# Layer 1's leaky slope: from VectorE in layer 2's edge stage to ScalarE and GpSimd in the first merge

## The reference

```
msg = x[src] @ W_msg + edge_attr @ W_edge
agg = segment_max(msg, dst); agg = 0 where a node has no edge
c   = leaky_relu(agg + x @ W_root + b)          # slope 0.01
```

## Time and profile before

| | |
|---|---|
| median of 3 runs | 2085.36 us (2079.59 to 2089.3) |
| the profiled execution | 2083.45 us, span 2081.6 us |
| mean granted TensorE clock | 0.914 |
| busy share | PE 78%, VectorE (DVE) 63%, GpSimd (POOL) 52%, ScalarE (ACT) 51% |

### The profile page before, as it was taken

One profiled execution on the slowest core, in us unless ns is written; L12 is line 12 of the kernel. 1 busy time (PEld: TensorE's weight loads), 2 busy tenths in 40 slices (PEclk: granted clock), 3 DMA queues, 4 the chain that ended last, 5 costly groups with the idle time before them and its releaser, 6 DMA issues.

```text
span 2081.6 us, 37108 instructions
## 1 busy us (share of the span) xinstructions
PE 1620.9 (78%) x11422; PEld 1408.5 (68%) x11422; DVE 1317.8 (63%) x2383; ACT 1056.0 (51%) x2450; POOL 1092.5 (52%) x1454
## 2 busy tenths in 40 slices
PE   3888888888888888886687888888888777666664
PEld 2657766667768888885566766676667666666664
DVE  2556666656666555553465655555654789999998
ACT  1323444334433455553344444443444678898897
POOL 6755666666640000002666666666664778766673
PEclk9988999999999999998899999889989989998887
DMA  6757888798874678885566766666767789999996
GB/s 122 187 132 217 232 240 230 214 243 229 231 222 176 203 237 261 271 279 188 142 183 181 196 189 185 191 188 177 197 182 233 221 268 294 306 301 291 297 293 195
DMA packets 580028, 459.13 MB, mean 221 GB/s; under 512 B 448559, under 2 KB 487346, under 8 KB 579842
## 3 DMA queue, kind: packets, MB, share of 16 engines
q1 hardware_dynamic: 497956, 301.88, 52.0%
q10 hardware_dynamic: 50910, 97.16, 12.6%
q0 software_dynamic: 30976, 57.72, 11.6%
HBM read 283.25 MB, written 173.37 MB: 219 GB/s over the span
## 4 chain that ended last, share of the span: by engine, by line
PE 52%; DVE 19%; another core or an unknown queue 10%; issue 10%; ACT 3%; POOL 3%; DMA 2%; ACTq 1%; SPq 1%; POOLq 0%; DVEq 0%
PE ps L556 17%; PE ps L468 14%; PE ps L459 8%; PE ps L437 6%; DVE stats L933 5%; PE ps L430 4%; DVE arena L931 3%; DVE arena L928 3%; PE ps L447 3%; POOL onehot L417 2%; DMA onehot_bytes<-arena 2%; DVE arena L951 1%; DVE arena L876 1%; ACT arena L620 1%
## 5 line engine op out<-in xcount | busy, mean ns | idle before, releaser
L556 PE MATMUL ps<-hold,onehot 128*128 x4688 | 610.6, 292 | 187.0 <-POOL onehot L417 136.9
L556 PEld LDWEIGHTS ps<-hold,onehot 128*128 128x128 f32 x4688 | 579.3, 204 | 218.4 <-issue 218.3
L384 POOL DMA_INDIRECT arena<-nodes,src_perm x392 | 370.8, 946 | 581.6 <-SPq L351 356.0
L468 PEld LDWEIGHTS ps<-w_root,onehot 97*128 97x128 f32 x3136 | 437.0, 209 | 170.0 <-issue 166.0
L468 PE MATMUL ps<-w_root,onehot 97*128 97x128 f32 x3136 | 460.3, 294 | 52.9 <-ACT arena L620 32.1
L384 POOL DMA_INDIRECT arena<-in_x_dram,src_all x392 | 377.7, 964 | 232.8 <-issue 115.0
L620 ACT COPY arena<-ps 128x384 f32<-128x384 f32 x392 | 188.2, 480 | 370.8 <-remote 241.3
L417 POOL CAST onehot<-keep 128x256 f32<-128x256 uint8 x588 | 302.2, 563 | 107.6 <-PE ps L556 64.5
L862 DVE TENSOR_TENSOR_SCAN arena<-keep,arena,ps 96x512 f32<-96x512 bf16 x196 | 248.3, 1267 | 142.1 <-remote 80.1
L459 PE MATMUL ps<-ident,arena 128*96 128x128 f32 x1568 | 262.3, 291 | 34.2 <-issue 27.7
L680 ACT COPY arena<-ps 128x384 f32<-128x384 f32 x392 | 166.7, 477 | 210.4 <-PE ps L556 210.4
(11 more groups left out here) (97 smaller groups left out, 1152.7 us busy)
## 6 DMA issues: line engine op xcount, KB each, us to landing
root<-arena ACTq DMA_DIRECT2D x196, 384.0 KB
arena<-root SPq DMA_DIRECT2D x196, 384.0 KB, 4.6
nodes<-arena SPq DMA_DIRECT2D x98, 384.0 KB, 2.8
arena<-nodes SPq DMA_DIRECT2D x98, 384.0 KB
arena<-in_x_dram SPq DMA_DIRECT2D x97, 384.0 KB
arena<-in_x_dram SPq DMA_DIRECT2D x48, 768.0 KB, 8.1
out_dram<-arena SPq DMA_DIRECT2D x48, 768.0 KB, 4.7
onehot_bytes<-arena ACTq DMA_DIRECT2D x147, 128.0 KB
```

The source lines that it names most:

```text
L384: nc.gpsimd.indirect_dma_start(out=gathered[t.ring][0:t.p, i, 0:D], out_offset=None, in_=table_in, in_offset=bass.IndirectOffsetOnAxis(ap= ...
L468: last = nc.tensor.matmul(no_ps[m % 2][:, i * P:(i + 1) * P], nodes_t[m % NODE_RING][0:D + 1, i * P:(i + 1) * P], w_root[0:D + 1, layer * ...
L556: nc.tensor.matmul(ps_bytes[:, bass.ds(place_at, SLOT)].bitcast(F32), onehot[:, k % NS, i, :], flat[:, bass.ds(chunk_at, P)], start=False, ...
```

## The change

Layer 1's result gets its slope before it is stored. `evacuate` makes two activations per node group from PSUM: `Relu(-0.01 x)` into a scratch half (`sloping`, in the place of `x_in[0]`, two halves) and `Relu(x)` into `nodes_out`. GpSimd then subtracts the first from the second, a half (128 x 768) at a time, and SyncE's store waits for that (`sloped`). ScalarE waits from the third half on until GpSimd has done the half two before. In edge stage 1 the operands are plain copies and VectorE's maxima are gone.

```diff
@@ sync: store_half
-                sp.wait_ge(evacuated[0], (h + 1) * HG)
+                sp.wait_ge(sloped, h + 1)
@@ gpsimd, between layer 1's gathers and the wait for ready
+            for h in range(2 * NSB):
+                pool.wait_ge(evacuated[0], (h + 1) * HG)
+                at = slice(h % 2 * HG * C * D, (h % 2 + 1) * HG * C * D)
+                y = nodes_out[h // 2 % 3][:, at]
+                nc.gpsimd.tensor_tensor(y, y, sloping[h % 2], ALU.subtract).then_inc(sloped, 1)
@@ scalar: read_edges
-                if t.layer == 0:
-                    nc.scalar.copy(to, of).then_inc(et_done, 1)
-                else:
-                    nc.scalar.activation(to, of, ACT.Copy, scale=slopes[:, 0:1]).then_inc(scaled, 1)
+                nc.scalar.copy(to, of).then_inc(et_done, 1)
@@ scalar: read_nodes
-                    nc.scalar.activation(to, of, ACT.Copy, scale=SLOPE).then_inc(nt_scaled, 1)
+                nc.scalar.copy(to, of).then_inc(nt_done, 1)
@@ scalar: evacuate
+                    if layer == 0 and h >= 2:
+                        act.wait_ge(sloped, h - 1)
...
+                        if layer == 0:
+                            off = n % HG * C * D
+                            nc.scalar.activation(sloping[h % 2][:, off:off + C * D]..., slot[:, n % RING, :, 0:D], ACT.Relu, scale=-SLOPE)
+                        nc.scalar.activation(nodes_out[s % 3][:, at:at + C * D]..., slot[:, n % RING, :, 0:D],
+                                             ACT.Copy if layer else ACT.Relu).then_inc(evacuated[layer], 1)
@@ vector: edge_phase
-                if layer == 1:
-                    leaky_edges(EdgeGroup(layer, 0))
...
-                    if layer == 1 and g + 1 < NE:
-                        leaky_edges(EdgeGroup(layer, g + 1))
...
-                            leaky_nodes(n)
```

More of the change, by code:

```diff
@@ L104, in gnn @@
         count = sb("count", [P, P], BF16)
-        slopes = sb("slopes", [P, 1], F32)
         rows = sb("rows", [ROWS_ON + 1, TP], I32)
@@ L125, in gnn @@
         x_in = [arena[:, UNIT_RING * UW + (3 + i) * SW:UNIT_RING * UW + (4 + i) * SW] for i in range(2)]
+        sloping = [x_in[0][:, i * HG * C * D:(i + 1) * HG * C * D] for i in range(2)]
         assert HG == UG and BATCH == 2 * C and NODE_RING == 2 * NS and EDGE_RING == 4
@@ L180, in gnn @@
         keep_in = sems("keep_in", EDGE_RING)
-        ones_set, turned, scaled, et_done, em_full, scanned, eb_full, held = (sem(n) for n in (
-            "ones_set", "turned", "scaled", "et_done", "em_full", "scanned", "eb_full", "held"))
-        block_in, nt_full, nt_scaled, nt_done = sems("block_in", UNIT_RING), sem("nt_full"), sem("nt_scaled"), sem("nt_done")
+        ones_set, turned, et_done, em_full, scanned, eb_full, held = (sem(n) for n in (
+            "ones_set", "turned", "et_done", "em_full", "scanned", "eb_full", "held"))
+        block_in, nt_full, nt_done = sems("block_in", UNIT_RING), sem("nt_full"), sem("nt_done")
+        sloped = sem("sloped")
         no_full, root_read, root_stored = sem("no_full"), sem("root_read"), sems("root_stored", UNIT_RING)
@@ L608, in read_nodes @@
                 to, of = nodes_t[m % NODE_RING][0:D, :], nt_ps[m % 2][0:D, :]
-                if layer == 0:
-                    nc.scalar.copy(to, of).then_inc(nt_done, 1)
-                else:
-                    nc.scalar.activation(to, of, ACT.Copy, scale=SLOPE).then_inc(nt_scaled, 1)
+                nc.scalar.copy(to, of).then_inc(nt_done, 1)
             def read_root(layer, n):
@@ L677, in evacuate @@
                     act.wait_ge(stepped[layer], ends[h % ENDS])
+                    if layer == 0 and h >= 2:
+                        act.wait_ge(sloped, h - 1)
                     for n in range(h * HG, (h + 1) * HG):
                         at = n % SG * C * D
-                        nc.scalar.copy(nodes_out[s % 3][:, at:at + C * D].rearrange("p (j d) -> p j d", d=D), slot[:, n % RING, :, 0:D],
-                                       ).then_inc(evacuated[layer], 1)
+                        if layer == 0:
+                            off = n % HG * C * D
+                            nc.scalar.activation(sloping[h % 2][:, off:off + C * D].rearrange("p (j d) -> p j d", d=D), slot[:, n % RING, :, 0:D], ACT.Relu, scale=-SLOPE)
+                        nc.scalar.activation(nodes_out[s % 3][:, at:at + C * D].rearrange("p (j d) -> p j d", d=D), slot[:, n % RING, :, 0:D],
+                                             ACT.Copy if layer else ACT.Relu).then_inc(evacuated[layer], 1)
                 def reseed(h):
@@ L736, in _ @@
             nc.vector.memset(end_prev, N - 1)
-            nc.vector.memset(slopes[0:D, :], SLOPE)
-            nc.vector.memset(slopes[D:K, :], 1.0)
             nc.vector.memset(ones, 1.0)
@@ L842, in _ @@
                 pieces[META_AT + 2 + k] = [lambda k=k: piece_pick(k)]
[L844 to L852, removed]
             def scan(t):
@@ L885, in edge_phase @@
             def edge_phase(layer):
-                if layer == 1:
-                    leaky_edges(EdgeGroup(layer, 0))
                 for g in range(NE):
-                    if layer == 1 and g + 1 < NE:
-                        leaky_edges(EdgeGroup(layer, g + 1))
-                    groups = node_groups(layer, g)
-                    for n in groups[0:1]:
-                        if layer == 1:
-                            leaky_nodes(n)
                     scan(EdgeGroup(layer, g))
@@ L897, in edge_phase @@
                         hold_chunks(EdgeGroup(layer, g - 1))
-                    for n in groups[1:]:
-                        if layer == 1:
-                            leaky_nodes(n)
                     if layer == 0:
```

## The result

The changed kernel takes 2115.31 us (median, 2114.7 to 2122.98) where the kernel before, on the same chip, takes 2085.34 us (2079.59 to 2089.3). The ratio is 1.0147, 95% interval 1.0112 to 1.0182: slower by 30 us. The profiled execution took 2114.7 us, span 2112.9 us, mean granted TensorE clock 0.914 as before.

A forecast was written before the change was run, and what follows sets the result against it. It took TensorE's matmuls to bound the first merge and the turn of four gathers and late TensorE signals the second edge stage. 2083.45 + 40.5 + 2.8 - 14 = 2112.8, so 2113 us, range 2035 to 2160 us.

The forecast's parts named there:

- the three terms: First merge +40.5 us, end of that merge +2.8 us, second edge stage -14 us.
- The subtraction's duration: First merge, GpSimd: one subtraction of 128x768 fp32 takes 1.8 us, between bounds of 1.05 and 2.1 us.
- Merge 0, +40.5 forecast: First merge: compares and subtractions exclude each other, 302.5 us of work in a 262 us stretch, +40.5 us.
- Rival C: First merge: the subtraction or the hand-overs are dear, merge +87 us, total 2159 us; chance 0.20.
- ScalarE beside TensorE: zero: First merge: two more Relu copies per half fit beside TensorE, 2.63 of 3.0 us, zero cost, at most 8 us.
- End of the merge, +2.8: After the first merge's last half: two more copies, one subtraction and signals before the store, +2.8 us.
- Edge stage 1, -14 forecast: Second edge stage: removing VectorE's maxima gains 0.15 us in each of 92 sets of gathers, -14 us.
- the hop on the turn (82 us): Second edge stage: VectorE's maximum is part of the turn, its removal gives 0.83 us a group, 82 us.
- four fifths of 0.19 us: Second edge stage: share of mean set minus undisturbed turn, for sets that narrowly missed the signal, 0.15 us a set.
- A: Second edge stage: the hop was on the turn, gain 82 us instead of 14, total 2045 us; chance 0.18.
- B: First merge: no lock between compare and subtraction, or a cheap one, +0 to 8 us, total 2076 us; chance 0.13.

The follow-up runs named there:

- e2_merge_only: Kernel before with the changed merge 0 (Relu copies and GpSimd subtraction), its layer 2 maxima kept: ratio 1.0133, merge 0 347.0 us.
- e3_relu_only: Changed kernel without GpSimd's subtraction, both Relu copies on ScalarE kept: ratio 1.001, merge 0 321.1 us.
- e4_write_only: Changed kernel with a GpSimd iota that only writes SBUF in the subtraction's place, without Relu(-0.01 x) copies: ratio 1.0024, merge 0 326.9 us.
- e5_sub_only: Changed kernel without the Relu(-0.01 x) copies, GpSimd subtracting what lies in the scratch: ratio 1.0198, merge 0 357.7 us.
- e1_edge_only: Changed kernel's edge stage 1 (plain copies, no maxima) with merge 0 of the kernel before: ratio 1.0002, edge stage 1 620.4 us.
- e9_half_sub: Changed kernel with the subtraction over 384 of 768 columns of each half: ratio 1.0071, merge 0 333.7 us.

## Why the prediction was right, and where its terms were off

**Mechanism.** Right. The cost is that the subtraction and the compare exclude each other (`e2_merge_only`, `e3_relu_only`, `e4_write_only`, `e5_sub_only`), the edge stage gives next to nothing back (`e1_edge_only`), and the total was 2115 for 2113 us. That the total came within 2 us is luck. Two terms were too large, with opposite signs, and left to themselves the three terms make +24.9 us in the traces where 29.3 were forecast; another 6.3 us came from stages that the change does not touch.

**The subtraction's duration.** 1.80 us was forecast, 1803 ns is the shortest of 98. It was a choice between 1.05 us for one operand and 2.1 us for two, and lay nearer to the second; no run has a GpSimd instruction that shows what a second operand costs by itself. In `e9_half_sub` 384 columns take 992 ns, so 384 more cost 0.81 us, and 0.18 us is there whatever the width. The estimate of 1.7 us from the Trainium skill, "GPSIMD Engine Reference", section "3.1 Elementwise — side-by-side cycle accounting", is 6% below the measurement.

**Merge 0, +40.5 forecast, +27.1 measured.** The sum took both instructions as excluding each other for their whole duration. They don't quite: 88 subtractions of 1.80 us and 121 compares of 1.22 us (700 to 990 us) are 306 us of work, and they ran in 290 us. The meetings above say where it comes from, 0.13 or 0.14 us at each change from one to the other. Over the whole merge it adds up to 25 us. If every instruction saved that, my own sum would have been 87 x 1.67 + 119 x 1.08 = 274 us in 262, 12 us more, and the least that the two can need in the stretch of 290 us is 88 x 1.67 + 121 x 1.08 = 278 us. The other error works against that: two such streams do not pack without holes. 119 compares now take 290 x 119 / 121 = 285 us instead of 262, so 23 us of the 27 come from this stretch and 4 from the 60 us before it, for which I had counted nothing. `e9_half_sub`, 12 us where the sum fits easily, shows this second part by itself. Rival C had named the holes as its argument; its price had them at full durations. One remark in the prediction is wrong, though no term rests on it: 98 subtractions of 1.8 us are 176 us and fit less than twice into the idle 326 us, not three times.

**ScalarE beside TensorE: zero.** Right; `e3_relu_only` has merge 0 at 321.1 us against 321.9. In the changed kernel's chain of waits GpSimd and ScalarE together have 1.1% of merge 0.

**End of the merge, +2.8.** Measured +2.7, and in its parts: the two copies alone make the hand-over 4.3 us instead of 3.5 (`e3_relu_only`), the subtraction alone 5.4 us (`e5_sub_only`).

**Edge stage 1, -14 forecast, -4.9 measured.** The choice between the hop on the turn (82 us) and off it was right, and the reason given (the first edge stage keeps the same pace without a hop) held. The mis-sized step is the "four fifths of 0.19 us" for sets that came late: nothing tied that rest to VectorE. The kernels whose layer 2 has no maxima and four gathers took 614.3 to 622.7 us for this stage, and `e2_merge_only` with all maxima 615.5 us, so even -4.9 us is not to be told from none.

**Other stages.** The +2.0 us in edge stage 0 and +4.3 us in merge 1 are not the change's: merge 1 takes 491 to 505 us in the twelve traces, and in `e1_edge_only` and `e3_relu_only` it is longer (498.7 and 502.1) than in the changed kernel.

**Rivals.** A fell to `e1_edge_only`, B to `e3_relu_only` against `e5_sub_only`; C named the right place, at three times the cost. No version here beats the kernel before by doing this change's work.

## What to carry to other kernels

Work given to an idle GpSimd is not free beside VectorE instructions that read two SBUF operands: count both engines' time in one sum if the GpSimd instruction reads SBUF, and expect a cost even where that sum fits (12 us at 85% of the stretch, 27 us at 96 to 105%). Cutting the GpSimd instruction into pieces only hands the wait to GpSimd (344.9 us against 349.0). An engine's removed work is worth what its stage's pace is worth: before taking 200 us off VectorE, find what repeats at the stage's period, here a set of four gathers, and change that alone as a test (-184 us). A sum that comes out within 2 us may still have two wrong terms; only stage marks of both traces show it.

## What the runs showed of the hardware

- A VectorE compare with two SBUF operands and a GpSimd subtraction exclude each other. Whichever starts second ends a fixed time after the other's end, however much they overlap: the compare 1.08 us (1.22 alone), the subtraction of 768 columns 1.67 us (1.80 alone), of 384 columns 0.86 us (0.99 alone, `e9_half_sub`).
- A GpSimd instruction that only writes SBUF (1.41 us, 89 times) leaves a two-operand compare at 1221 ns.
- Beside back-to-back indirect gathers TensorE's signals reach the other engines late: ScalarE's read 2.26 us after the transposes' end, in the lull after the fourth gather, and up to 4.41 us without a read beside eight gathers. With sets of two it is 0.04 us at the median of 89 reads. What in the gather path does this stays open.
